# Six PSUM banks for a weighted gather, and another order of its chunks in the repeated steps of a graph-network kernel

## The reference

```python
# layer 0
t1 = feat @ W1
msg = t1[src] + feat[src] * feat[dst] @ W2
msg = msg / (jnp.sqrt(out_deg[src]) * jnp.sqrt(out_deg[dst]))[:, None]
agg = jax.ops.segment_sum(msg, dst, num_segments=n)
embed = leaky_relu(jnp.where(in_cnt[:, None] > 0, t1 + agg, 0) + b)
embed = embed / jnp.maximum(norm(embed), 1e-12)
# layer 1
norm = dinv[row_sl] * ew_sl * dinv[col_sl]
msgs = (h @ W)[col_sl] * norm[:, None]
h7 = jax.ops.segment_sum(msgs, row_sl, num_segments=N) + b
out = relu(h7 @ W1 + b1) @ W2 + b2
```

## Time and profile before

| what | value |
|---|---|
| median of 3 runs | 2000.92 us (2000.2 to 2001.55) |
| the profiled execution's own time | 2004.59 us |
| its span, first to last instruction | 2000.5 us |
| TensorE busy | 1754.3 us, 88% |
| VectorE busy | 1262.9 us, 63% |
| GpSimd busy | 1083.3 us, 54% |
| ScalarE busy | 532.5 us, 27% |
| mean granted TensorE clock | 0.911 |

### The profile page before, as it was taken

One profiled execution on the slowest core, in us unless ns is written; L12 is line 12 of the kernel. 1 busy time (PEld: TensorE's weight loads), 2 busy tenths in 40 slices (PEclk: granted clock), 3 DMA queues, 4 the chain that ended last, 5 costly groups with the idle time before them and its releaser, 6 DMA issues. The chain is left out here.

```text
span 2000.5 us, 28981 instructions
## 1 busy us (share of the span) xinstructions
PE 1754.3 (88%) x10480; PEld 1120.0 (56%) x10480; DVE 1262.9 (63%) x1703; ACT 532.5 (27%) x854; POOL 1083.3 (54%) x1646
## 2 busy tenths in 40 slices
PE   4866976879989899888898699999998899999996
PEld 1244862227656576556575477577797354545453
DVE  6874747984443445353345235775656899999995
ACT  1400002004434353444354254350006111111111
POOL 4888888888888888878888883000000600000000
PEclk8955558889999899999899899999998999999998
DMA  9777874004353535353534355319760576667662
GB/s 346 302 287 306 319 273 158 10 1 133 100 197 110 187 129 167 102 194 99 177 120 132 112 178 171 105 57 336 229 217 14 172 247 208 226 224 229 203 229 80
DMA packets 254469, 354.47 MB, mean 177 GB/s; under 512 B 123879, under 2 KB 230044, under 8 KB 247837
## 3 DMA queue, kind: packets, MB, share of 16 engines
q1 hardware_dynamic: 138923, 306.98, 43.0%
q10 hardware_dynamic: 89654, 45.29, 7.7%
q0 software_dynamic: 25792, 0.88, 1.1%
HBM read 221.53 MB, written 131.55 MB: 176 GB/s over the span
## 5 line engine op out<-in xcount | busy, mean ns | idle before, releaser
L423 POOL DMA_INDIRECT table<-valT,idxT x806 | 777.6, 965 | 175.4 <-issue 149.3
L2268 DVE SCALAR_TENSOR_TENSOR wgt<-ratio,l3q,fcj 128x1664 f32<-128x1664 f32 (+1 forms) x195 | 365.8, 1908 | 27.6 <-PE psum L2312 18.4
L2308 PE MATMUL psum<-wgt,big 128*32 128x384 f32 (+1 forms) x3200 | 355.8, 495 | 7.8 <-DVE wgt L2268 7.8
L944 PE MATMUL psum<-region,g 128*128 128x512 f32 (+1 forms) x672 | 291.0, 580 | 35.5 <-DVE region L711 19.1
L944 PE MATMUL psum<-hx,region 128*128 128x257 f32 x1250 | 303.2, 386 | 11.9 <-ACT region L884 6.7
L421 POOL MEMSET rest<- 128x256 f32 x805 | 265.4, 330 | 1.7 <-DMA table<-valT,idxT 1.1
L702 DVE TENSOR_TENSOR big<-big,psum 128x512 f32<-128x512 f32 (+1 forms) x325 | 209.2, 664 | 89.0 <-PE psum L944 68.2
L944 PEld LDWEIGHTS psum<-hx,region 128*128 128x128 f32 x1250 | 229.8, 193 | 48.9 <-ACT region L884 11.5
L2312 PE MATMUL psum<-wgt,l3e 128*32 128x384 f32 (+1 forms) x1600 | 253.5, 494 | 0.0
L2308 PEld LDWEIGHTS psum<-wgt,big 128*32 128x32 f32 x3200 | 140.3, 110 | 143.6 <-issue 128.0
L944 PEld LDWEIGHTS psum<-region,g 128*128 128x128 f32 x672 | 125.3, 198 | 169.6 <-issue 153.4
(11 more groups left out here) (273 smaller groups left out, 1739.8 us busy)
## 6 DMA issues: line engine op xcount, KB each, us to landing
table<-tk SPq DMA_DIRECT2D x25, 3200.0 KB
tk<-table SPq DMA_DIRECT2D x25, 1664.0 KB
fcj<-counts_b SPq DMA_DIRECT2D x20, 2080.0 KB, 8.7
tk<-table SPq DMA_DIRECT2D x25, 1536.0 KB
fcj<-counts_b SPq DMA_DIRECT2D x19, 1920.0 KB, 7.8
counts_t<-region ACTq DMA_DIRECT2D x25, 800.0 KB
counts_b<-region ACTq DMA_DIRECT2D x25, 800.0 KB
table<-valT,idxT POOLq DMA_INDIRECT x806
```

The costliest lines, as they stand in the source:

```text
L423: eng.indirect_dma_start(out=table, out_offset=bass.IndirectOffsetOnAxis(idxT[:, c:c + 1], 0), in_=valT[:, c, :], in_offset=None).then_inc ...
L944: mm = lambda o, l, r_, st, sp: eng.matmul(o, l, r_, start=st, stop=sp, skip_group_check=True)
L2268: eng.scalar_tensor_tensor(out=tiles_of(wgt[:, n % NW, :]), in0=tiles_of(rb[:, p % 2, :]), scalar=qs[:, k, h:h + 1], in1=cj[:, m % NC, 0:n ...
L2308: eng.matmul(acc[p % 2][at:at + QUARTER, bank, 0:hi - lo], ftx[:, k, h, QUARTER * v:QUARTER * v + QUARTER], wgt[:, (NT * p + k) % NW, lo:h ...
```

## The change

The gather's chunks no longer share three banks. In a step with `cur` they use `WIDE`, banks 5, 6, 7, 2, 3, 4, 5, 6, 7, 4, 5, 6, 7 for chunks 0 to 12; in the closing step `NARROW`, the old banks. Chunk n waits for the lift of the last chunk that was in its bank (`lifted_first`). The transposes of the next tile wait for the lift of the last chunk that used their bank (`turn_next`). In the repeated steps `turn_g` and `fold` stand one group later, five chunks lie ahead of `turn_ab`, four between it and `dense`, and the last four chunks stand in between the next tile's groups: 9, group 0, 10, group 1, 11, 12, group 2. In the closing step the spread transposes wait for all lifts of the step before.

```diff
-        pL = psum[:, 5:8, :]
+        WIDE, NARROW = (5, 6, 7, 2, 3, 4, 5, 6, 7, 4, 5, 6, 7), (5, 6, 7) * 4 + (5,)
+
+        def lifted_first(banks, n):
+            same = [m for m in range(n) if banks[m] == banks[n]]
+            return same[-1] + 1 if same else 0
...
                 def lift(n):
                     j, z = prev
+                    at_bank = psum[:, (WIDE if cur else NARROW)[n], :]
...
             def step(cur, prev, last=False):
+                repeated = cur and not isinstance(cur[0], int)
...
-                        if prev and g == 2:
+                        if prev and g == (3 if repeated else 2):
                             turn_g(prev[0], g1)
-                        if prev and g == 4:
+                        if prev and g == (5 if repeated else 4):
                             fold(prev[0])
...
                 def gathered(chunks):
                     j, z = prev
                     of, g = (wt, g1) if cur else (tk[:, 0, :, :, 1], hk)
+                    banks = WIDE if cur else NARROW
                     for n in chunks:
-                        eng.wait_ge(sem("af"), 13 * j + max(n + 1, 3))
+                        eng.wait_ge(sem("af"), 3 + 13 * j + lifted_first(banks, n))
...
                 if prev and not cur:
                     turn_g(prev[0], hk)
+                    eng.wait_ge(sem("af"), 3 + 13 * prev[0])
                     for g, bank in enumerate(a.SPREAD_BANK):
...
+                def turn_next(g):
+                    if g == 0:
+                        eng.wait_ge(sem(f"tk{1 - s}0"), 16 * (r + s) + 16)
+                    if prev:
+                        eng.wait_ge(sem("af"), 3 + 13 * prev[0] + max(n for n in range(13) if WIDE[n] == 2 + g) + 1)
+                    turn(k + 1, 1 - s, g)
+                if repeated:
+                    gathered(range(0, 5))
+                    turn_ab()
+                    gathered(range(5, 9))
+                    dense()
+                    gathered([9])
+                    turn_next(0)
+                    gathered([10])
+                    turn_next(1)
+                    gathered([11, 12])
+                    turn_next(2)
+                    return
...
                 if not last:
-                    eng.wait_ge(sem(f"tk{1 - s}0"), 16 * (r + s) + 16)
                     for g in range(3):
-                        turn(k + 1, 1 - s, g)
+                        turn_next(g)
```

More of the change, by code:

```diff
@@ L696, in lift @@
                     j, z = prev
+                    at_bank = psum[:, (WIDE if cur else NARROW)[n], :]
                     if n < 12:
-                        part, more = acc[:, n % 2, 512 * (n // 2):512 * (n // 2) + 512], pL[:, n % 3, :]
+                        part, more = acc[:, n % 2, 512 * (n // 2):512 * (n // 2) + 512], at_bank
                     else:
-                        part, more = acc[:, :, 3072:NP], pL[:, 0, 0:2 * P].rearrange("p (o s) -> p o s", o=2)
+                        part, more = acc[:, :, 3072:NP], at_bank[:, 0:2 * P].rearrange("p (o s) -> p o s", o=2)
                     eng.wait_ge(sem("ag"), 13 * j + n + 2)
@@ L1081, in gathered @@
                     of, g = (wt, g1) if cur else (tk[:, 0, :, :, 1], hk)
+                    banks = WIDE if cur else NARROW
                     for n in chunks:
-                        eng.wait_ge(sem("af"), 13 * j + max(n + 1, 3))
+                        eng.wait_ge(sem("af"), 3 + 13 * j + lifted_first(banks, n))
                         if n < 12:
-                            mul = mm(pL[:, n % 3, :], g[:, n % 2 * P:n % 2 * P + P], of[:, 4 * (n // 2):4 * (n // 2) + 4, :], True, True)
+                            mul = mm(psum[:, banks[n], :], g[:, n % 2 * P:n % 2 * P + P], of[:, 4 * (n // 2):4 * (n // 2) + 4, :], True, True)
                         else:
                             for o in range(2):
-                                mul = mm(pL[:, 0, o * P:o * P + P], g[:, o * P:o * P + P], of[:, NT - 1, :], True, True)
+                                mul = mm(psum[:, banks[n], o * P:o * P + P], g[:, o * P:o * P + P], of[:, NT - 1, :], True, True)
                         mul.then_inc(sem("ag"), 1)
```

## The result

The changed kernel takes 2003.01 us (median of 18 runs, 2001.77 to 2007.24), the kernel before 1999.47 us (18 runs, 1996.96 to 2003.55). The ratio is 1.0018 [1.0011, 1.0025], so +3.5 us (2.2 to 5.0): inside the 0.2% that the forecast called the same, at its slow edge. The forecast was 2003.8 us, +2.85.

The account below looks back on a forecast made before the run. TensorE was taken as the bound, with tile 21's start set by GpSimd's scatters and hiding earlier losses. 2.15 + 0.70 = +2.85 us on the median of 2000.92 gave 2003.8 us, range 1999 to 2012.

Parts of the forecast that it names:

- part 5: GpSimd's pauses before scatters: loads could meet or miss one, moving tile 21's start by -4.0 to +4.0 us; taken as 0.
- part 1: New order inside repeated steps 1 to 20: +1.1 us a step, +22 us in all, hidden by 26.1 us idle.
- part 2: Step 20: chunks 10 to 12 now run behind the wait for tile 21's late load, +2.15 us.
- part 3: Unrolled steps 21 to 24: six banks free chunks 3 to 8, but TensorE does not wait there, 0 us.
- part 4: Closing step: the spread transposes now wait for every lift and start later, +0.70 us.
- (a): Repeated steps: `fold` one group later makes its result late for VectorE's diagonal add, 1.24 us of wait a step.
- (b): Repeated steps: fewer transposes between last chunk and products expose ScalarE's copy of group 3, 0.3 us, at most 1.1.
- The wait for `ab`: Repeated steps: TensorE's wait for `ab` is removed, since five chunks cover it, -0.2 us a step.
- the slack: TensorE's idle time before the loads of tiles 20 and 21, 26.1 us, said to hide the repeated steps' loss.
- The first rival: Slower: repeated steps use up the 26.1 us from 1.3 us a step; at 2 us a step 2012.7 us; 22%.
- that rival: Half-clock stretch behind the late load lasts until as much old work is done: moved chunks cost 4.3 us; 4%.
- The rival of one long pause more: Slower: one long GpSimd pause more delays tile 21, +4.0 us, 2007.8 us in all; 12%.

## Why the prediction was right, point by point

The mechanism was right: tile 21's start is GpSimd's date, what the repeated steps lose ahead of it is not seen, and most of the loss is the chunks behind the late load and the closing step's wait. That the sum comes within 0.7 us of the median is partly luck: parts 2 and 4 were 0.6 us too high together, and part 5, put at nothing, seems to hold about 1.3. The terms:

| term | forecast | measured |
|---|---|---|
| part 1, a repeated step | +1.1 us, hidden | +1.1 us (27.8 to 28.9), hidden |
| part 2, chunks behind the load | +2.15 us | +1.7 us |
| part 3, unrolled steps | 0 | 0 (83.62 us for three steps in every profile) |
| part 4, closing step | +0.70 us | +0.48 us |
| part 5, date of tile 21 | 0 (-4 to +4) | about +1.3 us, what is left of the sum, not settled |
| sum | +2.85 us | +3.5 us |

**Part 1.** The size was right, its make-up only in part. (a), the later fold, costs 0.7 us and not 1.24 (28.5 us a step with all chunks ahead of the transposes, 27.8 before). (b), the chunks between the transposes, costs the 0.3 it was given (28.5 to 28.9 us), but only while the fold is late: with the fold back the step is 27.8 us again. The wait for `ab` gave nothing, since TensorE had no such gap at 27.8 us a step. What failed is the slack: I read 26.1 us from the two load waits of one execution whose steps were 5 us too long. In the changed kernel's profile and the second one of before, seven and eight loads are late, 124 and 137 us in all. The first rival, which had 22% because 20 x 1.3 us would have used up 26.1, was therefore far from coming in: 124 / 20, some 6 us a step, would be needed (an estimate). That the misread slack did no harm is luck: it was wrong on the safe side. The loss of a step itself was real, and shows where GpSimd ends early.

**Part 2.** From the first transposes of tile 21 to `turn_ab` of step 21 it is 20.22, 19.67, 19.99, 20.26 and 19.50 us in the five profiles with all chunks ahead of the load, mean 19.93; with three behind it 21.27, 21.77 and 21.99, mean 21.68. That is 1.75 for the 2.15 that the chunks take at full clock. The rest is the half-clock stretch behind the wait. In the second profile of before, twelve transposes and four products take 1154.93 - 1149.57 = 5.36 us, where full clock needs 3.15 (the forecast's prices): 2.2 lost, at a mean granted clock of 0.57. In the changed kernel the same and 2.5 chunks take 1157.18 + 1.74 - 1151.96 = 6.96, where full clock needs 5.30: 1.7 lost, at a granted clock of 0.76. Over all eight profiles the means are 2.5 and 2.1, with single values of 2.0 to 2.8 and 1.7 to 2.4, so that the difference of 0.4 may be chance. So the stretch did not last until as much old work was done, and the 4.3 us of that rival, which would have raised the loss to some 4.6, are out; this is the side of the Trainium skill's page (TensorE: Matmul & The Clock Gate, Part 1), which calls the warm-up a time, and the traces agree to within 0.4 us.

**Part 4.** The wait is there, 1.13 us ahead of the spread transposes. But chunk 10 no longer waits 1.28 us for a lift, chunk 11 waits 0.43, so `turn_g` stands 11.47 us behind the transposes of `ab` (1268.32 - 1256.85) where with three banks it is 12.06 (1270.09 - 1258.03). The spread transposes stand 13.04 us behind them, against 12.27: 0.77 later, near the forecast's 0.70. Of that 0.48 is left at the end of the stage.

**Part 5.** The direct terms, 1.75 + 0.48 = 2.2, leave 1.3 of the 3.5 us. Of this result alone that is not clear of noise, since the interval begins at 2.2. All kernels with chunks behind the load are at 1.0017 to 1.0023, all with them ahead at 0.9998 to 1.0004, with or without the closing step's wait, so the rest seems to belong to that order too. The program behind the closing step does not hold it: it takes 711.7 to 712.3 us with chunks behind the load and 711.6 to 713.4 with them ahead. That leaves the date of tile 21: 1151.96, 1151.70 and 1152.42 us in the three profiles with chunks behind, against 1150.18, 1149.54 and 1149.57 in three with them ahead, yet 1152.53 in the fourth, the one with six banks and nothing moved, and 1153.80 in the execution shown before. Part of this scatter is older than the loop. One scatter behind a pause of GpSimd near 364 us, ahead of the loop, stands at 365.01 us in the profile with six banks and nothing moved, at 362.8 to 363.8 in the six others (364.53 in the execution shown before). Counted from it, tile 21 starts 788.2 to 788.9 us later with chunks behind and 786.1 to 787.5 with them ahead, 789.3 in the execution shown before, whose steps were held up. GpSimd's pause near 692 us goes along with it in part. Its timeline in the repeated changed kernel and in the repeated kernel before:

```profile
692.63 0.96 POOL L427 DMA_INDIRECT table<-valT,idxT  x1 [1.87 <-issue]
```

```profile
691.56 0.95 POOL L423 DMA_INDIRECT table<-valT,idxT  x1 [0.38 <-issue]
```

It is 2.10, 1.87 and 2.17 us with chunks behind, 1.68 and 1.57 with them ahead but the fold late, 0.38 in the repeated kernel before and with six banks and nothing moved, and 1.32 in the execution shown before. That the loads, issued at other times because of the steps' order, meet the pause is only argued: no run moved a load or a pause alone, and between single profiles the date varies by as much. The rival of one long pause more (+4.0) did not come in.

**What the profile was to show.** Tile 21's transposes lie 1.8 us from 1153.80, behind a wait of 16.9 us, with the chunks between them; SyncE issues that load 46.7 us after the one before (1098.25 and 1144.93); 28 us a step follow; the spread transposes wait for the last lift. Only "the steps before 1086 are about 1 us longer" can't be read against the profile of before, whose steps were 5 us too long; against the second one it holds.

**A version faster than both.** Without GpSimd's memsets the kernels are 6.2 and 6.6% faster than with them, and the changed one then needs only 3.3 us of waits for loads. The memset-free kernel with the fold back, which by the 1.1 us a step should gain again, wasn't tried.

## What to carry to other kernels

Work that stood ahead of a late transfer and is moved behind it costs most of its time (here 1.75 of 2.15 us), however well it fills the steps that don't wait; in a loop whose dates another engine sets, only the last such wait counts, and nothing shows of what the steps before it gain or lose. Before a slack is read from one profile, compare its step length with the sum of the bounding engine's work: where a step is longer and the waits say "remote" or "issue", that execution was held up, and a second profile is worth more than a finer reading of the first. And where an engine sets the dates, look first at what that engine does: here a memset that no one reads was worth 125 to 133 us, the whole reordering 3.5.

## What was not expected of the hardware

- VectorE's copies of TensorE's results can start up to 7.5 us (12.9 us on the chip of the four half-scatter runs) after the matmuls' recorded end, shown as "remote", where 0.04 us is the rule. It is seen only while GpSimd scatters; behind the last scatter the steps are regular to 0.1 us. One execution of the kernel before shows it and another doesn't, and the four half-scatter profiles, in either order of work, come from the chip on which the kernel before takes 2228 us and not 1999. Why stays open.
- GpSimd pauses before about every 112th scatter, at the same columns in every profile, for very different times: in eight profiles with the memsets 1.0 to 1.2 us near 1022 us, 4.4 to 5.2 near 858, 0.4 to 2.2 near 693, and near 528 1.0 to 2.0 in seven and 4.18 in the one shown before.
- Taking the 0.33 us memset out of a column saves 0.20 us, since the issue behind it takes 0.30 us in place of 0.17.
